# Third attention: a second copy of the split queries and keys in partitions 64 to 111, and two kinds of scores issued in turn

## The reference, cut to what matters

```python
q = (hidden_states @ Wq.T + bq) * SCALING
k = hidden_states @ Wk.T
v = hidden_states @ Wv.T + bv
q = q.reshape(bsz, tgt_len, NUM_HEADS, HEAD_DIM)
scores = jnp.einsum('bthd,bsd->bhts', q, k)
probs = jax.nn.softmax(scores, axis=-1)
ctx = jnp.einsum('bhts,bsd->bthd', probs, v)
ctx = ctx.reshape(bsz, tgt_len, EMBED_DIM)
return ctx @ Wo.T + bo
```

## Time and profile before

| | before |
|---|---|
| median of three runs | 3533.31 us (3531.64 to 3540.31) |
| the profiled execution's own time | 3533.18 us |
| its span, first to last instruction | 3530.9 us |
| mean granted clock of TensorE | 0.882 |
| TensorE busy, whole span | 2712.3 us (77%) |
| VectorE busy | 2145.8 us (61%) |
| ScalarE busy | 1307.7 us (37%) |
| GpSimd busy | 983.5 us (28%) |
| a2, maxima (L795), 256 | 168.1 us busy, 685 ns each |
| a2, exponentials (L569), 256 | 149.6 us busy, 596 ns each |

### The profile page before, as it was taken

How to read it: one execution, slowest core, us unless ns; L and a number is a source line. 1 busy time by engine, 2 the same in 40 slices (tenths; PEclk the granted TensorE clock), 3 DMA queues, 4 the chain that set the end, 5 groups by cost and what they waited for, 6 DMA issues and landing times. The chain is left out here.

```text
span 3530.9 us, 69910 instructions
## 1 busy us (share of the span) xinstructions
PE 2712.3 (77%) x20859; PEld 1810.2 (51%) x20884; DVE 2145.8 (61%) x5390; ACT 1307.7 (37%) x2884; POOL 983.5 (28%) x1089
## 2 busy tenths in 40 slices
PE   5888624317887887679849987788879998997999
PEld 3666524305665664528725555566634474455444
DVE  5776672137888786512247775777555567846455
ACT  1566201003665565324316663356432222133221
POOL 2332106852334332265622322334200020011000
PEclk6999756557999999889959998799989999998999
DMA  3332302334433331316521110333100004400000
GB/s 74 52 49 35 129 36 53 48 77 57 54 44 49 49 46 14 145 60 127 92 68 27 24 23 7 50 46 48 38 2 1 0 6 96 96 7 25 5 0 24
DMA packets 164036, 165.85 MB, mean 47 GB/s; under 512 B 30472, under 2 KB 136720, under 8 KB 158736
## 3 DMA queue, kind: packets, MB, share of 16 engines
q1 hardware_dynamic: 128240, 138.50, 20.4%
q0 software_dynamic: 34336, 21.83, 4.4%
q10 hardware_dynamic: 1152, 1.61, 0.1%
HBM read 52.90 MB, written 33.01 MB: 24 GB/s over the span
## 5 line engine op out<-in xcount | busy, mean ns | idle before, releaser
L569 ACT ACTIVATE a1PR<-bank 128x384 f32<-128x384 f32 x512 | 242.4, 492 | 143.6 <-PE bank L626 140.7
L792 DVE TENSOR_REDUCE a1NM<-bank 128x3 f32<-128x384 f32 x512 | 263.0, 549 | 26.6 <-PE bank L608 24.6
L795 DVE TENSOR_REDUCE a2NMQ<-bank 128x2 f32<-128x512 f32 x256 | 168.1, 685 | 60.8 <-PE bank L612 60.6
L959 PE MATMUL bank<-ONES 128*128 128x256 bf16 x960 | 169.5, 283 | 26.4 <-DMA f1nWR<-in_wr 5.0
L569 ACT ACTIVATE a2PR<-bank 128x512 f32<-128x512 f32 x256 | 149.6, 596 | 91.3 <-PE bank L630 89.2
L792 DVE TENSOR_REDUCE a4NM<-bank 128x3 f32<-128x384 f32 x256 | 136.1, 552 | 57.0 <-PE bank L608 55.3
L792 DVE TENSOR_REDUCE a0NM<-bank 128x3 f32<-128x384 f32 x256 | 136.6, 553 | 50.2 <-PE bank L608 47.4
L624 PE MATMUL bank<-a1QH,a1KH 128*128 128x128 bf16 x512 | 115.6, 227 | 57.4 <-ACT a1PR L569 43.1
L569 ACT ACTIVATE a4PR<-bank 128x384 f32<-128x384 f32 x256 | 121.2, 489 | 97.5 <-PE bank L626 96.6
L569 ACT ACTIVATE a0PR<-bank 128x384 f32<-128x384 f32 x256 | 119.9, 489 | 82.7 <-PE bank L626 82.0
L2208 POOL DMA_INDIRECT routed<-yY,yID x80 | 123.6, 1545 | 85.7 <-DMA routed<-yY,yID 41.4
(11 more groups left out here) (675 smaller groups left out, 8334.9 us busy)
## 6 DMA issues: line engine op xcount, KB each, us to landing
lVB<-lV SPq DMA_DIRECT2D x64, 256.0 KB
yWT<-in_w SPq DMA_DIRECT2D x40, 256.0 KB, 3.0
a1QH<-a1SPL SPq DMA_DIRECT2D x96, 64.0 KB
a1KH<-a1SPL SPq DMA_DIRECT2D x96, 64.0 KB
a1QH<-a1QH SPq DMA_DIRECT2D x96, 64.0 KB
a1KH<-a1KH SPq DMA_DIRECT2D x96, 64.0 KB
rows_by_slot<-gZB SPq DMA_DIRECT2D x5, 1040.0 KB
yXG<-rows_by_slot SPq DMA_DIRECT2D x40, 130.0 KB, 3.1
```

The costliest lines, as they stand in the source:

```text
L569: nc.scalar.activation(PR[:, h % 8, :], bank[2 + h % 2][:, 0:NC], ACT.Exp, scale=SCALE)\
L792: v.tensor_reduce(NM3[:, h, :], S_BANK[h % 3][:, 0:NC].rearrange("p (n k) -> p n k", n=3), AX, ALU.max, negate=True).then_inc(s_used.sem, 1)
L795: v.tensor_reduce(NMQ[:, :, h], S_BANK[h % 3][:, 0:NC].rearrange("p (n k) -> p n k", n=2), AX, ALU.max, negate=True).then_inc(s_used.sem, 1)
L959: pe.matmul(bank[7][:, 0:2 * P], spare[:, 0:P], spare[:, :], start=True, stop=True)
```

## The change

The attention gets an option `halves`, set for a2 alone. With it QH and KH have 112 rows. Rows 64 to 111 hold a copy of rows 0 to 47: SyncE waits, after its fourteen DMAs, until the ten that `parts_sent` counted have landed, and issues two more, one for the queries' 48 rows and one for the keys'. TensorE's wait before the block's scores is for all twelve that count there now. The maxima's scores are computed from rows 64 to 111, the exponential's from rows 0 to 49. Where a slot has both, a new function issues them in turn, half by half, after the waits of both. VectorE no longer fills row 64 and beyond: two fills per buffer remain of four.

```diff
+    halves = cfg.get("halves")
+    COPY = 64 if halves else 0
-    KROWS = P if causal else FREE
+    KROWS = P if causal else COPY + ROWS if halves else FREE
+    FILLS = 2 if halves else 4
...
-parts_sent=16 * 10
+parts_sent=16 * (12 if halves else 10)
...
+                        if halves:
+                            after(sp, parts_sent[r], b, 16 * 10)
+                            sp.dma_start(QH[COPY:COPY + ROWS, j, :, :], QH[0:ROWS, j, :, :]).then_inc(parts_sent[r].sem, 16)
+                            sp.dma_start(KH[COPY:COPY + ROWS, j, :, :], KH[0:ROWS, j, :, :]).then_inc(parts_sent[r].sem, 16)
...
+            def scores_pair(t, m, p, b, j, h):
+
+                scores_t_ready(t, p)
+                scores_ready(b, h)
+                KP, QP = KH[0:ROWS + 2, m, kof(head(p)), :], QH[0:ROWS + 2, m, head(p), :]
+                KS, QS = KH[COPY:COPY + ROWS, j, kof(h), :], QH[COPY:COPY + ROWS, j, h, :]
+                for n in range(2):
+                    mt = pe.matmul(bank[2 + p % 2][:, n * T:(n + 1) * T], KP[:, n * P:(n + 1) * P], QP, start=True, stop=True)
+                    ms = pe.matmul(S_BANK[h % 3][:, n * T:(n + 1) * T], QS[:, n * P:(n + 1) * P], KS, start=True, stop=True)
+                mt.then_inc(st_ready.sem, 1)
+                ms.then_inc(s_ready.sem, 1)
...
-                    k = KH[0:FREE, j, kof(h), :]
-                    pe.matmul(o[:, 0:T], q(0), k, start=True, stop=True)
-                    mm = pe.matmul(o[:, T:2 * T], q(1), k, start=True, stop=True)
+                    KS, QS = KH[COPY:COPY + ROWS, j, kof(h), :], QH[COPY:COPY + ROWS, j, h, :]
+                    for n in range(2):
+                        mm = pe.matmul(o[:, n * T:(n + 1) * T], QS[:, n * P:(n + 1) * P], KS, start=True, stop=True)
...
                 for h in range(NH):
-                    if has(0, t):
+                    due = [(a, n) for a, n in scored_at(h) if has(a, t)]
+                    if halves and has(0, t) and due:
+                        a, n = due.pop(0)
+                        scores_pair(t, m, h, t + a, (m + a) % LEAD, n)
+                    elif has(0, t):
                         scores_t(t, m, h)
-                    for a, n in scored_at(h):
-                        if has(a, t):
-                            scores(t + a, (m + a) % LEAD, n)
+                    for a, n in due:
+                        scores(t + a, (m + a) % LEAD, n)
...
-        attention_phase(c, dict(ln, name="a2", ..., causal=False,
+        attention_phase(c, dict(ln, name="a2", ..., causal=False, halves=True,
```

More of the change, by code:

```diff
@@ L335, in attention_phase @@
                     xn_ready=1, h_ready=1, qk_ready=QK, qk_copied=QK, half_ready=int(bool(rope)), rope_ready=int(bool(rope)),
-                    hi_ready=R, res_ready=R, mid_ready=R, lo_ready=R, high_sent=32, mid_sent=32, parts_sent=16 * 10, high_sent_1=32 * (R - 1), mid_sent_1=32 * (R - 1), parts_sent_1=16 * 8 * (R - 1),
+                    hi_ready=R, res_ready=R, mid_ready=R, lo_ready=R, high_sent=32, mid_sent=32, parts_sent=16 * (12 if halves else 10), high_sent_1=32 * (R - 1), mid_sent_1=32 * (R - 1), parts_sent_1=16 * 8 * (R - 1),
                     v_ready=1, v_copied=1, s_ready=NH, s_used=NH, nmq_ready=4 * int(causal), mt_ready=2, mhi_ready=2, mlo_ready=2, go=2,
@@ L442, in step @@
                     sp.wait_ge(zeroed, 2)
-                    sp.wait_ge(rows_ready, 4 * (t + LEAD - 1) + 2)
+                    sp.wait_ge(rows_ready, FILLS * (t + LEAD - 1) + 2)
                 if has(LEAD - 1, t):
@@ L594, in _, with scores_ready @@
                 pe.wait_ge(gate_ready, 1)
-            def scores(b, j, h):
+            def scores_pair(t, m, p, b, j, h):
[8 more added lines that the diff above has]
+                ms.then_inc(s_ready.sem, 1)
+            def scores_ready(b, h):
                 after(pe, s_used, b, max(h - 2, 0))
@@ L600, in scores @@
                 if h == 0 and isinstance(b, int) and b < LEAD:
-                    pe.wait_ge(rows_ready, 4 + 4 * b)
+                    pe.wait_ge(rows_ready, FILLS + FILLS * b)
+            def scores(b, j, h):
+                scores_ready(b, h)
                 o = S_BANK[h % 3]
@@ L609, in scores, with scores_t_ready @@
                 else:
-                    k = KH[0:FREE, j, kof(h), :]
-                    pe.matmul(o[:, 0:T], q(0), k, start=True, stop=True)
-                    mm = pe.matmul(o[:, T:2 * T], q(1), k, start=True, stop=True)
+                    KS, QS = KH[COPY:COPY + ROWS, j, kof(h), :], QH[COPY:COPY + ROWS, j, h, :]
+                    for n in range(2):
+                        mm = pe.matmul(o[:, n * T:(n + 1) * T], QS[:, n * P:(n + 1) * P], KS, start=True, stop=True)
                 mm.then_inc(s_ready.sem, 1)
-            def scores_t(b, j, p):
+            def scores_t_ready(b, p):
                 after(pe, p_ready, b, p - 1)
@@ L618, in scores_t @@
                     after(pe, m_sent[p // HG], b)
+            def scores_t(b, j, p):
+                scores_t_ready(b, p)
                 h = head(p)
@@ L627, in scores_t @@
                 else:
-                    q = QH[0:FREE, j, h, :]
-                    pe.matmul(o[:, 0:T], k(0), q, start=True, stop=True)
-                    mm = pe.matmul(o[:, T:2 * T], k(1), q, start=True, stop=True)
+                    KP, QP = KH[0:ROWS + 2, j, kof(h), :], QH[0:ROWS + 2, j, h, :]
+                    for n in range(2):
+                        mm = pe.matmul(o[:, n * T:(n + 1) * T], KP[:, n * P:(n + 1) * P], QP, start=True, stop=True)
                 mm.then_inc(st_ready.sem, 1)
@@ L744, in fill @@
                     v.wait_ge(rows_in, 32)
-                for part in parts:
+                for part in parts[:FILLS]:
                     rows = (slice(32, 64), slice(64, KROWS))[part // 2]
@@ L890, in step @@
                             turned(t - back, (m - back) % LEAD, s)
-                    for part in range(4 if isinstance(t, int) and t < -1 else 0):
+                    for part in range(FILLS if isinstance(t, int) and t < -1 else 0):
                         if h == L_FILL[part]:
@@ L2329, in build @@
                            w1="w1_1", w2="w2_1", ybias="yb1", ebias="eb1"))
-        attention_phase(c, dict(ln, name="a2", lead=3, first_score=0, score_slots=13, nmq=(8, 13), layer=2, NH=16, HK=1, HV=1, VW=8, CW=128, causal=False,
+        attention_phase(c, dict(ln, name="a2", lead=3, first_score=0, score_slots=13, nmq=(8, 13), layer=2, NH=16, HK=1, HV=1, VW=8, CW=128, causal=False, halves=True,
                                 bq="bq2", bv="bv2", bo="bo2", wq="wq2", wk="wk2", wv="wv2", wo="wo2", src=c.XT, dst=c.XT))
```

## The result

| | before | after |
|---|---|---|
| median | 3533.56 us (4 runs) | 3590.64 us (4 runs, 3581.77 to 3599.72) |
| ratio to before | | 1.0158, 95% interval 1.0123 to 1.0193 |
| the profiled execution's own time | 3533.18 us | 3583.68 us |
| its span | 3530.9 us | 3581.4 us |
| mean granted clock | 0.882 | 0.870 |

What follows compares the result with a forecast made beforehand. TensorE was nearest to full, but a loop from slot 0 through projections and copies would bind. First block 4.49, second 3.44, thirteen steady 14.0, last 2.91: + 24.8 us on 3533.2 gives 3558; range 3539 to 3590.

Steps and rivals of the forecast that it cites:

- first mechanism: Third attention: late copies lengthen the loop from slot 0 to slot 0; added latency 4.49 us against 3.28 us slack.
- forecast at + 1.08: Each of thirteen steady blocks of the third attention grows by 1.08 us, 14.0 us together.
- the far bound: Copies' bytes: 384 KB at the second attention's rate per engine, on all 16 DMA engines, take 3.15 us.
- The start: First two blocks of the third attention: copies add 4.49 us in the first and 3.44 in the second.
- TensorE's gain: Paired half-array scores save at most 2.9 us per block, shape switches cost 1.35; net 1.5, hidden by the wait.
- the paragraph on the copies: SyncE's wait and two copies cost only latency, 4.49 us added (3.44 to 5.54, far end 8.69).
- rival D: Slot 0's new wait may drop the clock to 0.50 in every block: 13 x 1.5 on top, 3578 us; chance 0.08.
- forecast + 2.91: Last block of the third attention: added latency less slack of 1.58 us makes it 2.91 us longer.
- A: Copies land before they are needed, so TensorE's 1.5 us per block count: faster, 3521.5 us; chance 0.04.
- B: No change: the large copy is as quick as the small one, 3.44 us; + 8.1, 3541 us; chance 0.12.
- C: Much slower: the copies' eight-row groups follow each other, 8.69 us added latency; + 92, 3625 us; chance 0.12.
- E: Scores of 50 rows still take the whole array and pairs don't overlap: 1.7 us more, 3560 us; chance 0.04.

Runs made afterwards that it cites:

- e12: Changed kernel with only the first eight heads' maxima taken in slot 7 in place of 8: 3578.64 us, ratio 1.0111.
- e3: Changed kernel with copies of 8 rows in place of 48: 3603.85 us, ratio 1.017.
- e10: Kernel before the change, with only the first eight heads' maxima taken in slot 7 in place of 8: 3526.81 us, ratio 0.9970.
- e8: As e5, with the first eight heads' maxima taken in slot 7 in place of 8: 3534.13 us, ratio 0.9999.
- e6: As e1, but neither TensorE nor ScalarE waits for the copies, which nothing reads: 3579.92 us, ratio 1.0115.
- e4: Changed kernel with twelve idle matmuls at the end of slot 15, before slot 0's wait: 3567.78 us, ratio 1.0094.
- e9: As e5, with six idle matmuls in each of two TensorE waits per block: 3561.3 us, ratio 1.0060.
- e5: Changed kernel, parts sent straight to rows 64 to 111, copies to rows 0 to 47 issued after the maxima's rows land, cast not waiting for them: 3574.47 us.
- e1: Changed kernel with scores as before, unpaired; the copies (to unread rows) and the waits for them kept: 3586.54 us, ratio 1.0157.

## Why the prediction was right or wrong

**Direction and first mechanism: right.** The loop from slot 0 over the projections, SyncE's list and the copies back to slot 0 is late once two more copies stand behind a wait. From the last group's key copy to the scores the prediction had 2.78 + 4.49 = 7.27 us; e12 shows 1926.07 to 1933.63, 7.56. The steady block, forecast at + 1.08, is + 1.40 in e12. The split was otherwise: SyncE waits 2.69 to 3.00 us where 2.2 were taken, and 4.56 in place of 5.1 pass from there to the scores; the bytes' 1.05 stand (e3), though the far bound behind them, 3.15, doesn't follow from its row: 6.3 us at 44% of the engines are 2.8. The start, 4.49 + 3.44 = 7.93, measured 8.23.

**TensorE's gain: right.** Net 1.5 us per block forecast, 1.38 measured (15.32 for 16.70). It was put at nothing, because the wait covers it. "Were it gone they would count" did not come out: e10 beside e8 shows that without the wait, too, the gain is worth 0.10 us a block.

**The step that failed** is in the paragraph on the copies: "Behind that wait on SyncE stands only the next block's sequence, which cannot start before its own cast; the cost is latency." That looked at SyncE's own queue alone. The copies also meet GpSimd's maxima rows on the DMA engines, and those set slot 0 already before the change, with 0.34 us of waiting in the earlier trace rows: the row was read as a short wait, not as a second loop with no slack. It runs from slot 0 over the scores of eight heads, their maxima and the two small DMAs back to slot 0. e6 shows it alone, e12 the other loop alone. In the steady blocks it changed the size little (20.15 with both, 19.97 and 20.00 with one), but the way back: no cure of the copies' lateness alone could work. The Trainium skill says (DMA: Bandwidth & Descriptors, Queues, rings and completion order) that each DMA engine serves the queues it has work for in turn, a packet at a time. The trace agrees in kind: 1.6 us alone, 3.4 beside the copies, with packets that start later and are no longer.

**The term that was mis-sized** is the clock, rival D, held at 0.08 and kept out of the sum. It came, though not in every block: 13 x 1.53 (20.10, the median of the five blocks at full clock, less 18.57, the median before) is 19.9 of the steady 27.6 us; the remaining 7.7 go with a clock of 0.91 for 0.97. At the end, forecast + 2.91, 12.7 of 14.97 us are longer busy time at 0.69 for 0.99. So of some 26 us in a2 that the sum lacked, about 6 are longer steady blocks at full clock (19.9 for 14.0), and about 20 stand in the stretches with a lower clock (7.7, and 12.1 at the end). Rival D had + 20 over the forecast, 3578; the profiled execution took 3583.68. The earlier trace rows showed the pattern, and the row deserved more than 0.08: the forecast itself put idle time into every block. That the clock is a cause and not only a companion is what e4 (23 us less by idle matmuls) and e9 (shorter falls, less time) speak for; how much of the 50 us is its alone stays open, since fillers also lengthened blocks, and since each pattern of falls here was read from one execution of its kernel. In e5 no block escaped the falls, so its 18.2 us at full clock was never seen.

**The other rivals.** A and B are out by the time. C is out by the added latency: 7.56 less 2.78 is 4.78 us in e12, where C had 8.69. E is out: pairs start together, 0.11 us apart from the next.

## What to carry to other kernels

Before costing a DMA, list what else is on the DMA engines when it will be under way, and who waits for that: bytes that nobody waits for can cost as much as bytes that somebody does. A short wait at the head of a step (0.34 us here) can mark a second loop without slack; here one slot earlier for the maxima was worth more than faster scores, to the kernel before as well (a ratio of 0.997, at the edge of what was measured). Where two late loops end together, take both away in one experiment, or each seems to cost nothing.

## What the runs showed that was not expected

- Two DMAs of 4 KB from GpSimd's queue take 1.6 us from issue to landing by themselves and 3.1 to 3.4 beside 0.42 MB of copies on SyncE's queue.
- In e5 less work went with a worse clock: with 1.4 us less of matmuls per block, its waits for VectorE grew from at most 0.8 and 0.6 us to 1.22 and 1.03, and the granted clock fell to 0.50 in every second block; one slot earlier for the maxima (e8) ended both from 1936.80 to 2121.12 us. With the scores as before the clock fell too (e1, e6), beside a slot 0 that waits for the maxima's rows.
- A fall is not the same each time: 3.41 us in most steady blocks of the changed kernel that have one, 10.24 in e5, and 34.13 us once each in e1 and e6, where a whole block ran at 0.50 (29.82 us in e1).
